# Attention with score tiles regrouped: four in a row per set of value matmuls, exponentials over two PSUM banks with three groups in flight

## What is computed

```python
mod = (jnp.cos(quantum_phase) * quantum_amplitude)[None, :, None, :]
q, k, v = (proj(W) * mod for W in (Wq, Wk, Wv))   # 16 heads of width 8
scores = jnp.einsum('bhid,bhjd->bhij', q, k) / math.sqrt(D)
scores = scores * cos_mat                          # cos(2 pi (i - j) / S)
w = jax.nn.softmax(scores, axis=-1)
w = (w + jnp.roll(w, 1, axis=-1)) / math.sqrt(2.0)
out = jnp.einsum('bhij,bhjd->bhid', w, v)
return out.transpose(0, 2, 1, 3).reshape(B, S, d) @ Wo
```

## Time and profile before

| | |
|---|---|
| median of 3 runs | 768.14 us (767.87 to 769.38) |
| the profiled execution, its own time | 767.0 us |
| its span | 765.3 us, so 1.7 us lie around it |
| first exponential of attention | 209.38 us |
| last exponential of attention | 749.25 us |
| PE busy | 622.2 us, 81% |
| ACT busy | 546.5 us, 71% |
| DVE busy | 220.8 us, 29% |
| exponentials (L578) | 342, 467.6 us busy |
| score matmuls (L1078) | 1024, 896 of them in the first 14 heads |
| value matmuls (L1094) | 256 quads, 2048 records |
| maximum jobs (L1112) | 128, and as many reductions (L768) |

### The profile page before, as it was taken

The page is one execution under the profiler, slowest core; times in us unless marked ns, Lnnn a source line. Parts: engine busy times, 40 slices in busy tenths (PEclk is TensorE's granted clock), DMA queues, the critical chain, the costliest instruction groups (busy, mean ns, idle before and its releaser), DMA issues.

```text
span 765.3 us, 11470 instructions
## 1 busy us (share of the span) xinstructions
PE 622.2 (81%) x4151; PEld 213.8 (28%) x4152; DVE 220.8 (29%) x462; ACT 546.5 (71%) x530; POOL 93.3 (12%) x109
## 2 busy tenths in 40 slices
PE   4991187999888888888888989888888888878886
PEld 3840055777611111111111111111111111111113
DVE  7785033444300222231322222222222222005002
ACT  1555031333489888988888787888888888898992
POOL 1058600111101010101011010101010000000000
PEclk9996586999989999999999999999999999999999
DMA  5925120111321010101001010101011010000002
GB/s 140 324 68 186 68 83 27 56 55 52 108 62 36 8 42 1 42 1 43 19 24 36 7 43 1 42 1 42 1 43 33 8 32 1 3 0 1 1 1 58
DMA packets 33828, 34.44 MB, mean 45 GB/s; under 512 B 6092, under 2 KB 27878, under 8 KB 33650
## 3 DMA queue, kind: packets, MB, share of 16 engines
q1 hardware_dynamic: 30786, 27.01, 12.1%
q0 software_dynamic: 2992, 6.76, 2.7%
HBM read 21.14 MB, written 12.58 MB: 44 GB/s over the span
## 4 chain that ended last, share of the span: by engine, by line
PE 60%; ACT 23%; issue 7%; POOL 5%; DVE 4%; DMA 1%; ACTq 0%; DVEq 0%; POOLq 0%
PE ps L1094 26%; ACT big L578 22%; PE ps L1078 13%; POOL slots_x L441 5%; PE ps L978 4%; PE ps L1112 4%; PE ps L971 4%; PE ps L983 3%; PE ps L961 2%; PE ps L1101 1%; PE ps L903 1%; PE ps L912 1%; PE ps L956 1%; PE ps L1053 1%; PE ps L895 1%
## 5 line engine op out<-in xcount | busy, mean ns | idle before, releaser
L578 ACT ACTIVATE big<-ps 128x1536 f32<-128x1536 f32 x342 | 467.6, 1456 | 72.9 <-PE ps L1078 70.9
L1094 PE MATMUL ps<-big,vh 128*32 128x512 f32 x2048 | 271.4, 613 | 0.0
L1078 PE MATMUL ps<-qa,ka 49*128 49x512 f16 x896 | 164.8, 384 | 68.1 <-ACT big L578 64.8
L768 DVE TENSOR_REDUCE m<-ps 128x1 f32<-128x512 f32 x128 | 88.5, 691 | 213.0 <-PE ps L1112 213.0
L1078 PEld LDWEIGHTS ps<-qa,ka 49*128 49x128 f16 x896 | 37.2, 94 | 181.3 <-ACT big L578 145.2
L1094 PEld LDWEIGHTS ps<-big,vh 128*32 128x32 f32 x2048 | 43.6, 109 | 103.4 <-issue 101.4
L433 POOL COPY vh<-vaug 128x144 f32 x16 | 5.1, 316 | 435.4 <-PE ps L1094 434.1
L1112 PE MATMUL ps<-ka,attnT 49*128 49x512 f16 x128 | 49.9, 390 | 0.0
L735 DVE TENSOR_TENSOR cs<-pair,ps 128x352 f32<-128x352 f32 x39 | 20.3, 521 | 87.2 <-PE ps L983 83.6
L550 ACT COPY y<-ps 128x128 f32<-128x128 f32 x39 | 10.4, 266 | 47.9 <-PE ps L971 47.9
L1112 PEld LDWEIGHTS ps<-ka,attnT 49*128 49x128 f16 x128 | 11.8, 92 | 109.5 <-issue 109.5
(11 more groups left out here) (165 smaller groups left out, 369.7 us busy)
## 6 DMA issues: line engine op xcount, KB each, us to landing
qk_parts<-store SPq DMA_DIRECT2D x16, 256.0 KB
qa<-qk_parts SPq DMA_DIRECT2D x28, 128.0 KB
slots_x<-vh SPq DMA_DIRECT2D x5, 512.0 KB, 9.1
cs<-slots_x SPq DMA_DIRECT2D x20, 128.0 KB, 2.2
slots_y<-y POOLq DMA_DIRECT2D x19, 128.0 KB, 2.6
store<-in_L_ffn_w SPq DMA_DIRECT2D x4, 512.0 KB, 6.5
ka<-qk_parts SPq DMA_DIRECT2D x32, 64.0 KB, 2.0
qa<-qk_parts SPq DMA_DIRECT2D x28, 64.0 KB
```

The costliest lines, as they stand in the source:

```text
L578: nc.scalar.activation(probs[:, first % PROBS:first % PROBS + n, :], ps[:, first % RING:first % RING + n, :], ACT.Exp, scale=ISQ8 / (OPERA ...
L768: nc.vector.tensor_reduce(m4[:, j // NC, j % NC:j % NC + 1], ps[:, O_BANKS[(p - 1) % 2], :], AX, ALU.max).then_inc(m_reduced, 1)
L1078: ins = nc.tensor.matmul(ps[:, n % RING, :], k[at:at + KQ, P * o:P * o + P], q[at:at + KQ, CW * c:CW * c + CW], start=True, stop=True, til ...
L1094: ins = nc.tensor.matmul(ps[32 * c:32 * c + 32, O_BANKS[p % 2], :], vh[:, p % 2, k // 2 + 8 * (k % 2), :], probs[:, n % PROBS, :], start=k ...
```

## The change

Groups have two tiles in place of three, the ring has three groups in place of two (6 banks either way), and `probs` 16 tiles in place of 15. `scores(g)` waits for the exponential of group g-3. Inside an eight the query chunk is 0, 1, 2, 3, 1, 0, 3, 2 while `b` goes on alternating, so that every four tiles in a row have four different chunks and form one quad; the value matmuls of a quad then take the weights of two key tiles. The quad of four tiles runs two groups after its last group. Jobs are no longer placed behind quads: from quad 6 of a head on, each pass of the group loop makes one job, between the scores and the quad. The order of the jobs within a key tile is 2, 0, 3, 1.

```diff
@@ -57,9 +57,9 @@
-GROUP_OF = 3
-RING = 2 * GROUP_OF
-PROBS = 5 * GROUP_OF
+GROUP_OF = 2
+RING = 3 * GROUP_OF
+PROBS = 8 * GROUP_OF
...
+JOB_QUAD = 6
...
         def tile_at(n):
 
             p, r = n // PER_HEAD, n % PER_HEAD
-            return p, r // 8, r % 8 // 2, r % 2
+            s = r % 8
+            return p, r // 8, s if s < NC else s - NC ^ 1, r % 2
 
         def tiles_of_quad(q):
 
-            first = q // QUADS * PER_HEAD + q % QUADS // 2 * 8 + q % 2
-            return [first + 2 * c for c in range(NC)]
+            return range(NC * q, NC * q + NC)
...
         def quads_for(n):
 
-            p, o, c, b = tile_at(n - 1)
-            whole_octs = p * QUADS + 2 * o
-            return whole_octs + (1 if (n - 1) % 8 == 0 else 2)
+            return (n - 1) // NC + 1
+
+        def job_at(j):
+
+            return j // PER_HEAD, j // NC % NT, (2, 0, 3, 1)[j % NC]
...
             def scores(g):
 
-                after(pe, exp_done, g - 1)
+                after(pe, exp_done, g - 2)
...
-                for c, n in enumerate(tiles):
-                    ins = nc.tensor.matmul(ps[32 * c:32 * c + 32, O_BANKS[p % 2], :], vh[:, p % 2, k // 2 + 8 * (k % 2), :],
+                for n in tiles:
+                    _, o, c, b = tile_at(n)
+                    ins = nc.tensor.matmul(ps[32 * c:32 * c + 32, O_BANKS[p % 2], :], vh[:, p % 2, o + 8 * b, :],
                                            probs[:, n % PROBS, :], start=k == 0, stop=k == QUADS - 1, tile_position=(0, 32 * c))
...
-                j = jobs_before(p) + k - 4
-                if 4 <= k and j < jobs_before(p + 1):
-                    max_job(p, j)
...
-            w = 0
-            for g in range(SCORE_GROUPS + 2):
+            w, j = 0, 0
+            for g in range(SCORE_GROUPS + 3):
                 if g < SCORE_GROUPS:
                     scores(g)
-                while w < H * QUADS and tiles_of_quad(w)[-1] < (g - 1) * GROUP_OF:
+                if w % QUADS >= JOB_QUAD and j < jobs_before(w // QUADS + 1):
+                    max_job(w // QUADS, j)
+                    j += 1
+                while w < H * QUADS and tiles_of_quad(w)[-1] < (g - 2) * GROUP_OF:
                     weighted_values(w)
                     between(w)
                     w += 1
```

More of the change, by code:

```diff
@@ L1104, in max_job @@
             def max_job(p, j):
-                r, i, c = j // PER_HEAD, j // NC % NT, j % NC
+                r, i, c = job_at(j)
                 if j == 0:
```

## The result

The changed kernel takes 742.93 us in the median of four runs (741.48 to 744.86). The kernel before took 768.0 in the median of four runs (762.21 to 769.38), and the ratio is 0.969, with a 95% interval of 0.964 to 0.974: 3.1% faster. The forecast was 740 us and a range of 721 to 758.

A forecast was written before the change was run, and what follows sets the result against it. Two engines, ACT and PE, hand work back and forth, neither full; afterwards ACT bounds. 209.4 + 466.4 + 0.1, jobs 40, clock 2 + 5 and the end gave 738.2 us of span, 739.9 with 1.7 around it: 740 us, range 721 to 758.

The forecast's parts named there:

- first exponential: Time up to ACT's first exponential of attention, kept as in the kernel before: 209.4 us.
- 512 exponentials: ACT's own work in attention: 512 exponentials of 1024 columns at a pitch of 0.911 us, 466.4 us.
- jobs: Attention heads with jobs: PE waits for DVE between job pairs, 2.69 us per two groups against 1.82; 40 us together.
- clock, start of attention: PE at half clock for some us as attention starts, delaying ACT: 2 us kept (0 to 4).
- clock, inside attention: Short stretches of PE at half clock within attention, expected again because of pauses among the jobs: 5 us (0 to 30).
- behind the last exponential: End after ACT's last exponential: DVE's copy starts 1.1 us behind, then 14.2 us to the end as before.
- ACT's 72.9 us of idle time: ACT's idle time in attention before the change, which is what the change can win.
- One sign that I gave: Sign for the exponential line L581: a mean near 1.03 us and a pitch near 0.91.
- the hand-over from DVE to PE: Within the job-to-job time of 1.17 us: from the end of DVE's reduction to PE, 0.05 us.
- The slower rival: PE's clock falls in job stretches: 818 us if all at half clock; chance 0.08 slower, shared with no overlap on ACT.

The follow-up runs named there:

- e1: Changed kernel with each job behind a quad again, one a quad: 696.34 us, ratio 0.913 to the kernel before.
- e4b: Changed kernel with one more reduction of 256 columns on DVE ahead of each job's own: 762.71 us, ratio 1.000 to the kernel before.
- e8: Changed kernel with one job per pass still, but behind the quad of the pass instead of ahead of it: 740.32 us, ratio 0.968 to the kernel before.
- e7: Changed kernel with one job a quad, placed between the scores and the quad: 695.77 us, ratio 0.910 to the kernel before.
- e0: Changed kernel again, unedited, on the same chip as e4b: 742.52 us, ratio 0.975 to the kernel before.
- e3: Kernel before with groups of two, three in flight, 16 buffers, old tile order, jobs behind quads: 756.40 us, ratio 0.992 to the kernel before.
- e5: e1 with two groups of two in flight in place of three: 733.36 us, ratio 0.961 to the kernel before.
- e6: e2 with the four transposes of the head before moved to a pass without a quad: 704.95 us, ratio 0.924 to the kernel before.
- e2: Kernel before with the new order of tiles alone, groups of three, two in flight, jobs behind quads: 707.88 us, ratio 0.929 to the kernel before.
- e9: Kernel before, unedited, profiled on another chip in one execution: 765.46 us.

## Why the prediction was right

Term by term, for the profiled execution, which was the slowest of the four and lies 5.0 us above the sum (743.2 of span against 738.2):

| term | forecast | measured | from |
|---|---|---|---|
| first exponential | 209.4 | 210.6 | timeline of ACT |
| 512 exponentials | 466.4 | 469.4 | pitch 0.917, not 0.911 |
| jobs | 40 | 44.8 | 11 heads of 3.9, and head 12 |
| clock, start of attention | 2 | 1.5 | 7 exponentials in 7.88 us, not 6.4 |
| clock, inside attention | 5 | 0 | granted clock 1.00 |
| behind the last exponential | 15.3 | 16.9 | 726.30 to 743.2 |

**The exponential** was sized from two other shapes and came out 0.006 us off. ACT's 72.9 us of idle time fell to 40.0: what it had lost to two quads in a row went as forecast, heads without jobs have no gap, and what is left is new and comes from the jobs. By the rule of the Trainium skill, "ScalarE: Activation LUTs", section "What ACT_TABLE_LOAD costs", the pitch was estimated at 0.946 us; the trace has 0.917, nearer to the 0.911 of the rows. One sign that I gave fails: the mean of L581 is not near 1.03 but 1.18 us, and 1.44 in e1, at the same pitch. Group of this line in the changed kernel:

```profile
L581 ACT ACTIVATE big<-ps 128x1024 f32<-128x1024 f32 x512 | 475.7, 1179 | 40.0 <-PE ps L1081 40.0
```

**The jobs** were the step on which the forecast turned: 2.69 us a double group, 2.78 measured, 58 waits for DVE as counted, a break before every second exponential. Mis-sized was the hand-over from DVE to PE. I took 0.05 us from a copy that PE waited for; from the end of the reduction (290.50 + 0.69) to the job's matmul (291.33) it is 0.14. Five short intervals a head make 0.45 us of it, and with that the difference from 3.5 to 3.9. e4b made the wait longer and the time followed, e8 moved it within the pass and the time stayed near the change's; e1 and e7 removed it and 46 us went.

**The clock inside attention** was the wrong term, and its reason was wrong too. I kept 5 us for it, and far more in a rival, because PE would pause among the jobs, "more regularly than before". The changed kernel has none inside attention, nor has any of e0 to e8, though the changed kernel and e8 pause 0.66 us in every double group, and e4b 0.99. And its pauses are not more but fewer: 58 waits for DVE and 2 for ACT, 38.7 us, where the kernel before has 98 waits of its score matmuls for ACT, 75.8 us, up to 1.7 long. The Trainium skill's rule ("TensorE: Matmul & The Clock Gate", Part 1), that activity releases the throttle, isn't contradicted by this. But what I took from it, that more pauses mean more falls, is: e3 has 130 such waits, 83.5 us in all (0.69 us each in its stretches with jobs, 1.26 once at the start), and no fall inside attention. Which property of the old order brings the falls stays open. The slower rival thus had no part in the result.

**Behind the last exponential** the forecast took the time of before, and that hid a clock term. The output projection is the same work in both kernels; here are its first 16 matmuls before:

```profile
754.75 2.05 PE L1053 MATMUL ps<-wo_mod,attnT 128*128 128x128 f32 x16 [0.24 <-ACT attnT L585]
```

and after:

```profile
731.10 3.33 PE L1056 MATMUL ps<-wo_mod,attnT 128*128 128x128 f32 x16
```

In the changed kernel the granted clock is 0.50 from 730.4 to 733.8 us, in the kernel before it is 1.00 from the last quad to 763.2. Among the kernels here, this end takes 16.5 to 16.9 us in the profiles with such a fall (after, e0, e1, e5, e6) and 15.3 to 15.5 in those without (before, e2, e4b, e7, e8, e9); e3 has none and takes 16.2, with two quads left in place of one. So the 1.6 us that the table has too little there are mostly clock, in a place where none was forecast. The first row of the table differs by as much between two profiles of one kernel: in e0 the first exponential is at 207.2 us, 3.3 earlier.

So the number came out well in part by luck: 5.5 us too much for the clock at the start and inside attention and some 10.5 too little for the other terms partly cancel, and the median lies 1.9 us below the profiled execution, where I had put it 1.1 above the one of before. The step that carried the forecast, the 40 us of the jobs, is right in its mechanism and 4.8 us short.

## What to carry to other kernels

When a ring of buffers starves its consumer, look first at the longest piece of work that the producer does between two of its groups. In this kernel spreading it (the order of tiles, 54 us) was worth far more than smaller groups (5 us). A round trip through a third engine is free only while something as long as the trip stands between its two ends in the waiting engine's order: pairs of jobs with 0.2 us between them cost 46 us, on an engine with time to spare. Price an operation that is issued more often by its pitch in an unbroken row, not by its mean length.

## What had not been expected of the hardware

The recorded length of a 128x1024 exponential grows in a row in which ACT never waits, and its pitch does not. Behind a wait it is 1.02 us, and each further one of the row is some 13 ns longer, with a few steps back, up to 1.67. So the mean is 1.03 us in e3, where PE only just delivers, and 1.44 in e1, while a full row has 0.917 from one to the next in both the changed kernel and e1 ((463.02 - 1.02) / 504 = 0.917). The records of a well-fed ACT overlap more and more, and neither their mean nor their overlap prices an instruction.

Inside attention the kernel before falls to half clock three times at the same places of its program on two chips, and a fourth time on the second, and each fall costs ACT about 1.6 us; none of the nine other programs here (the change and e1 to e8) did so inside attention, while some fell in the projection behind it.
